# An attention and feed-forward layer on eight cores: the feed-forward weights quantised with their input channels on the partitions

## The chip, the cores and the metric

The kernel runs on all 8 NeuronCores of one Trainium2 chip, each on its own 1024 of the 8192 tokens; no core waits for another. The time is that of the slowest core, in microseconds (us). The engines are TensorE (PE: matmuls and, by matmul with an identity, transposes), VectorE (DVE), ScalarE (ACT), GpSimd (POOL, here only an issuer of DMAs) and SyncE (SP, the other issuer of DMAs). Each runs its own list of instructions in order and waits on semaphores.

## The reference

With D = 2048 channels and 16 heads of 128, cut to what matters:

```
x = x + attention(layernorm(x), w_qkv) @ w_proj.T      # softmax over the 16 heads of one token
z  = layernorm(x)
xq = fake_quant(z, 8, axis=-1)         # scale = max|.| / 127, round(z / scale) * scale
kq = fake_quant(kernel, 8, axis=0)     # one scale for each OUTPUT channel, over all input channels
y  = relu(xq @ kq + fake_quant(bias))
x  = x + fake_quant(y, 8, axis=-1)
```

`kernel` is [2048 input channels, 2048 output channels] in float32. Its quantised form `kq` depends on no activation, so each core can make it any time before the last matmuls.

## The kernel before

**Start.** SP loads the 8 token tiles (128 tokens x 2048, 1 MB each). VectorE takes the statistics of a tile, ScalarE normalises it to bf16 (`abuf`), TensorE transposes it in two halves of 8 blocks (`a_transpose`), and `at_evac` copies the first half by VectorE and the second by ScalarE to `aT`. Batches of small matmuls on zeros (`warm`, L938) fill the waits of TensorE between the first tiles. Job 0 starts on tiles 0 to 2 (`q_tiles(0, 0, 3)`), then does tile 3.

**Projection.** 96 jobs: job (e, h) multiplies weight block e of 48 (q, k and v, 16 blocks each) with half h of the tokens, 16 matmuls of 512 columns. POOL loads the weight blocks through six buffers `wqb` with a cast to bf16, block e as soon as the jobs of block e-6 are done, so about 12 jobs ahead. Results lie in five PSUM banks in turn; VectorE evacuates the even jobs, ScalarE the odd ones. In POOL's list the chunks of the output projection's weights (`wpq`) are mixed in.

**Weight quantisation, beside the projection.** Between evacuations, panel by panel: 16 panels of 128 rows of the transposed kernel, so that an output channel lies on one partition and its scale is one number per partition. A panel takes three jobs from job 10 on: VectorE `k_scale` (absolute maximum over 2048, scale, reciprocal), ScalarE `k_round` (multiply and round, in place), VectorE `k_quant` (back to bf16), then SP spills it to DRAM (`kr_spill`).

**Attention.** TensorE runs slots, written out by the loop `for sl in range(NS)`: in slot `sl` the scores of group sl (32 groups), the transposes of sl-1, the product with V of sl-2, and beside them 16 matmuls of the jobs left over (slots 0 to 5), of the output projection (slots 6 to 37, tile b in slots 6+4b to 9+4b) or of the feed-forward product (`y_part`, from slot 38). SP's list holds, in this order and for one after the other: the DMA transposes of V (`v_transpose`, V of tile b), the loads of the residual (`xres_load`, into the space of K and V that are done with; VectorE adds to it in `p_evac`), twelve DMA transposes of the spilled panels (`k_transpose`, which POOL writes back to `kq_spill`), four more straight into `kq[0]` (`kq0_transpose`), the DMA transposes of the quantised activations (`l_transpose`), and then the bias and the loads of `kq[1]`, `kq[2]`, `kq[3]` (`kq_load`, 2 MB each). `kq[1]` to `kq[3]` take the space of `wpq`, so `kq_load(u)` waits for product 28+u of 32 of the output projection.

**Feed-forward.** 32 products `y_part(k, u)` of 16 matmuls; the four of tile k use the four quarters `kq[0]` to `kq[3]` in turn. Then VectorE and ScalarE quantise each tile, and SP stores it.

## Time and profile before

| | us |
|---|---|
| three timed runs | 642.28, 643.17, 647.33 (median 643.17) |
| the profiled execution | 647.92 |
| its span on the slowest core (core 5) | 646.4 |
| spans of cores 0 to 7 | 645.4, 640.6, 636.3, 643.0, 640.5, 646.4, 639.7, 633.5 |
| mean granted TensorE clock of cores 0 to 7 | 0.977, 0.980, 0.988, 0.982, 0.980, 0.981, 0.986, 0.989 |
| TensorE busy on core 5 | 608.7 (94%) |
| VectorE, ScalarE busy on core 5 | 316.8 (49%), 239.4 (37%) |
| on the chain that ended last | TensorE 67%, SP's DMA issues 23% |

The profiled execution lasted 1.5 us longer than the span of its slowest core. TensorE is busy nearly all the time, so the microseconds that can move are those in which it waits or runs at its lower clock. All cores run the same program on equal amounts of work, yet their spans lie 13 us apart; comparing them stage by stage tells which waits made the slow ones slow.

### The profile page before, as it was taken

What the parts mean: (1) busy time and instruction counts of PE and PEld (TensorE: products, weight loads), DVE (VectorE), ACT (ScalarE), POOL (GpSimd) and SP (SyncE); (2) the same over time, 40 slices, a digit from 0 to 9 for tenths busy, and PEclk for the clock granted to TensorE, in tenths of its full rate; (3) what the DMA queues carried; (4) which work ended last, traced back from release to release, by engine and by line L of the source; (5) the groups of instructions that cost most, each with busy time, mean ns of one, the idle gap of its engine ahead of it and who ended that gap; (6) DMA issues with size and microseconds to landing.
All of it is one profiled execution on the core that took longest, in us unless ns stands there. A gap on an engine that the chain in (4) does not pass through costs nothing.

```text
span 646.4 us, 9466 instructions; the slowest of 8 cores (633.5 to 646.4 us)
## 1 busy us (share of the span) xinstructions
PE 608.7 (94%) x3416; PEld 302.7 (47%) x3416; DVE 316.8 (49%) x492; ACT 239.4 (37%) x492; POOL 41.0 (6%) x80
## 2 busy tenths in 40 slices
PE   5789999999999999999999999999979979999993
PEld 5645444444444444444444555554544424444442
DVE  3853445435354340010012456867748635778657
ACT  3862123221331320100002667675647323453331
POOL 0100100000000011111100000000000000000000
PEclk8899999999999999999999999999989999999997
DMA  8998789999999999999834989999999992332313
GB/s 243 268 202 209 158 207 231 199 255 221 228 227 222 248 175 163 165 151 157 119 61 60 184 143 244 199 179 196 147 251 207 260 321 60 98 97 106 122 66 130
DMA packets 88974, 116.02 MB, mean 179 GB/s; under 512 B 69089, under 2 KB 69089, under 8 KB 85217
## 3 DMA queue, kind: packets, MB, share of 16 engines
q1 hardware_dynamic: 77986, 75.58, 46.2%
q0 software_dynamic: 10944, 39.85, 37.5%
q8 instruction: 28, 0.46, 0.3%
q14 instruction: 16, 0.13, 0.1%
HBM read 109.12 MB, written 23.08 MB: 205 GB/s over the span
## 4 chain that ended last, share of the span: by engine, by line
PE 67%; SPq 23%; DMA 6%; DVE 2%; issue 1%; ACT 1%; DVEq 0%; ACTq 0%; POOLq 0%
PE pF L804 49%; PE pF L909 16%; SPq L263 11%; SPq L253 4%; SPq L240 3%; SPq L272 3%; DMA wqb<-wqkv 2%; DMA xbuf<-x_att 2%; DMA kq<-kq_spill 2%; DVE cols L536 1%; SPq L247 1%; PE pF L928 1%; PE pF L822 1%; ACT aT L403 0%; ACT abuf L397 0%
## 5 line engine op out<-in xcount | busy, mean ns | idle before, releaser
L804 PE MATMUL pF<-aT,wqb 128*128 128x512 bf16 x1504 | 327.1, 379 | 2.0 <-DMA wqb<-wqkv 2.0
L804 PEld LDWEIGHTS pF<-aT,wqb 128*128 128x128 bf16 x1504 | 146.5, 98 | 176.2 <-issue 2.3
L886 PE MATMUL pF<-wpq,qT 128*128 128x512 bf16 x512 | 120.9, 382 | 0.0
L909 PE MATMUL pF<-kq,xqT 128*128 128x512 bf16 x496 | 108.8, 382 | 4.8 <-DMA kq<-kq_spill 3.6
L909 PEld LDWEIGHTS pF<-kq,xqT 128*128 128x128 bf16 x496 | 48.6, 98 | 65.1 <-issue 7.9
L886 PEld LDWEIGHTS pF<-wpq,qT 128*128 128x128 bf16 x512 | 48.1, 99 | 48.1 <-issue 1.6
L428 ACT ACTIVATE Ebuf<-pF,cols 128x128 bf16<-128x128 f32 x128 | 45.6, 369 | 40.7 <-DVE cols L598 39.6
L560 DVE CAST vT<-pF 128x512 bf16<-128x512 f32 x16 | 11.0, 690 | 80.8 <-PE pF L804 80.8
L354 POOL DMA_DIRECT2D wqb<-wqkv x48 | 26.0, 541 | 295.5 <-PE pF L804 244.3
L560 DVE CAST kT<-pF 128x512 bf16<-128x512 f32 x16 | 11.1, 692 | 63.0 <-PE pF L804 63.0
L661 DVE SCALAR_TENSOR_TENSOR tt<-pF,cols,bqb 128x512 f32<-128x512 f32 x31 | 23.2, 750 | 38.1 <-PE pF L909 37.9
L415 ACT CAST vT<-pF 128x512 bf16<-128x512 f32 x16 | 9.4, 588 | 83.0 <-PE pF L804 83.0
L415 ACT CAST kT<-pF 128x512 bf16<-128x512 f32 x16 | 9.4, 587 | 80.1 <-PE pF L804 80.1
L557 DVE TENSOR_SCALAR qT<-pF 128x512 bf16<-128x512 f32 x16 | 11.1, 691 | 55.2 <-PE pF L804 49.1
L584 DVE TENSOR_REDUCE cols<-wkf 128x1 f32<-128x2048 f32 x16 | 36.4, 2277 | 0.0
L412 ACT ACTIVATE qT<-pF 128x512 bf16<-128x512 f32 x16 | 9.6, 599 | 71.9 <-PE pF L804 71.9
L419 ACT ACTIVATE wkf<-wkf,cols 128x2048 f32<-128x2048 f32 x16 | 32.0, 2003 | 5.3 <-DVE cols L566 5.3
L468 ACT ACTIVATE tt<-tt,cols 128x2048 f32<-128x2048 f32 x7 | 14.0, 2003 | 48.1 <-DVE cols L566 48.1
L617 DVE TENSOR_TENSOR xr<-pF,xr 128x512 f32<-128x512 f32 x32 | 21.9, 684 | 15.9 <-DMA xr<-x_res 11.2
L598 DVE TENSOR_REDUCE cols<-pF 128x4 f32<-128x512 f32 x32 | 22.0, 688 | 14.5 <-PE pF L844 14.5
L428 ACT ACTIVATION_READ_ACCUMULATOR Ebuf<-pF,cols 128x1 f32 x128 | 26.3, 206 | 0.0
L449 ACT ACTIVATE zb<-xr,cols 128x1024 f32<-128x1024 f32 x16 | 18.6, 1161 | 17.8 <-DVE qx L651 17.8
...
## 6 DMA issues: line engine op xcount, KB each, us to landing
wqb<-wqkv POOLq DMA_DIRECT2D x48, 512.0 KB, 8.6
...
kr_spill<-kqr SPq DMA_DIRECT2D x16, 512.0 KB, 11.3
wpq<-wp POOLq DMA_DIRECT2D x16, 512.0 KB, 9.6
...
kq_spill<-kst POOLq DMA_DIRECT2D x12, 512.0 KB, 8.8
```

The costliest lines, as they stand in the source:

```text
L253: inc(sync.dma_start_transpose(xqT[:, 2048 * b:2048 * (b + 1)].rearrange("p (c n) -> p c n", c=NC), qx[:, :]), f"lT{b}", 16)
L263: inc(sync.dma_start_transpose(kst[i % 5].rearrange("p (c n) -> p c n", c=NC), d_kr[512 + 128 * i:512 + 128 * (i + 1), :]), f"kT{i % 5}", 16)
L354: inc(g.dma_start(wqb[e % NW][:, :], d_wqkv[128 * e:128 * (e + 1), :]), f"wL{e % NW}", 16)
L419: inc(s.activation(wkf[ft % 2][:, :], wkf[ft % 2][:, :], AF.Copy, bias=MAGIC, scale=cc(C_KR[ft])), "kZ")
L428: i = s.activation(Ebuf[g % 2][:, cs], pF[3 + g % 2][:, cs], AF.Exp, bias=cc(C_NM[g % 2] + j), accum_out=cc(C_DEN[g % 2] + j))
L560: inc(v.tensor_copy(qkv_dst(e, h), qkv_src(j)), "qEvV")
L584: h = inc(v.reduce_max(cc(C_KA[ft % 2]), wkf[ft % 2][:, :], AX.X, apply_absolute_value=True), "vS")
L598: inc(v.tensor_reduce(cc(C_NM[g % 2], 4), pF[3 + g % 2].rearrange("p (j n) -> p j n", j=4), AX.X, ALU.max, negate=True), "vMx")
L661: return inc(v.scalar_tensor_tensor(tt[k % 2][:, cs], pF[(4 * k + u) % 4][:, :], cc(C_SX[k]), bqb[:, cs], ALU.mult, ALU.add), "yEv")
L804: mm = tn.matmul(pF[QBANK[j]][:, :], wqb[e % NW][:, 128 * c:128 * (c + 1)], aT[:, 8192 * h + 512 * c: 8192 * h + 512 * (c + 1)], start=(c ...
L886: mm = tn.matmul(pF[SLOTB[f % 3]][:, :], sT[:, 2048 * b + 128 * m: 2048 * b + 128 * (m + 1)], wpq[u][:, 512 * m:512 * (m + 1)], start=(m = ...
L909: mm = tn.matmul(pF[y % 4][:, :], xqT[:, 2048 * k + 128 * c: 2048 * k + 128 * (c + 1)], w[:, c, :, :], start=(c == 0), stop=(c == NC - 1))
```

## The change

The kernel matrix comes in another layout from the host: panel ft holds, on partition p, the 128 output channels n with their 16 input blocks c side by side, so the input channels lie on the partitions. A quantised panel is then already what `y_part` reads. All 16 DMA transposes of panels, `kr_spill` and POOL's twelve write-backs go; SP writes each panel to `kq_spill`, and `kq[0]` is loaded like the others. An output channel's maximum now goes over partitions: VectorE reduces to `kM`, transposes 32x32 blocks, reduces, gathers four lanes, and spreads scale and reciprocal back over all partitions (`kRow`); the multiplication by the reciprocal is a VectorE instruction (`k_mult`), ScalarE only rounds, reading with a stride of 16 elements into a new buffer `wkz`. Panels start at job 4 and take four jobs each, and `k_quant` of a panel stands at the start of the next panel. The buffers move to the space of `wpq[0]` to `wpq[2]`, so the `wpq` loads are spread anew, and POOL waits for the last spills before that of block 39. The residual is loaded from ScalarE's list, after the exponentials of slot 4b+3. At the start, tile 2 is copied by VectorE alone, tile 3 is transposed after `q_tiles(0, 0, 3)`, and one `warm` batch is gone.

```diff
...
-PREP0 = 10
+PREP0, PREPN = 4, 4
...
+WP_WITH = {20: (0, 0), 23: (0, 1), 26: (1, 0), 29: (1, 1), 39: (0, 2), 40: (0, 3),
+           41: (1, 2), 42: (1, 3), 43: (2, 0), 44: (2, 1), 45: (2, 2), 46: (2, 3)}
...
+    wkf = [A(f"wkf{i}", [128, 2048], F32, offset=163840 + 8192 * i)
            for i in range(2)]
-    kqr = [A(f"kqr{i}", [128, 2048], BF16, offset=114688 + 4096 * i)
+    kqr = [A(f"kqr{i}", [128, 2048], BF16, offset=155648 + 4096 * i)
            for i in range(2)]
+    wkz = A("wkz", [128, 2048], F32, offset=139264)
...
-            sync.wait_ge(S_("qMM"), 3)
-            inc(sync.dma_start(wkf[1][:, :], d_bias.partition_broadcast(128)),
+            sync.wait_ge(S_("qMM"), 4)
+            inc(sync.dma_start(wkf[0][:, :], d_wk[0:128, :]), "kL0", 16)
+            inc(sync.dma_start(wkf[1][:, :], d_wk[128:256, :]), "kL1", 16)
+            sync.wait_ge(S_("qMM"), 5)
+            inc(sync.dma_start(bia[:, :], d_bias.partition_broadcast(128)),
...
             sync.wait_ge(S_("bQ"), 1)
-            inc(sync.dma_start(d_bq[:, :], wkf[1][0:1, :]), "bSt", 16)
-            sync.wait_ge(S_("bSt"), 16)
-            inc(sync.dma_start(wkf[1][:, :], d_wkT[128:256, :]), "kL1", 16)
+            inc(sync.dma_start(d_bq[:, :], bia[0:1, :]), "bSt", 16)
             for ft in range(NC):
-                sync.wait_ge(S_("kQ"), ft + 1)
+                sync.wait_ge(S_("kZ"), ft + 1)
                 if ft + 2 < NC:
                     inc(sync.dma_start(
                         wkf[ft % 2][:, :],
...
-                inc(sync.dma_start(d_kr[128 * ft:128 * (ft + 1), :],
-                                   kqr[ft % 2][:, :]), f"kSp{ft % 2}", 16)
...
+                u, f4 = ft // 4, ft % 4
+                sync.wait_ge(S_("kQ"), ft + 1)
+                inc(sync.dma_start(
+                    d_kq[128 * u:128 * (u + 1), 2048 * f4:2048 * (f4 + 1)],
+                    kqr[ft % 2][:, :]), f"kSp{ft % 2}", 16)
...
-            def k_transpose(i):
-                if i == 0:
+            def kq_load(u):
+                if u == 0:
+                    sync.wait_ge(S_("kSp0"), 128)
+                    sync.wait_ge(S_("kSp1"), 128)
                     sync.wait_ge(S_("qMM"), NJ)
-                if i >= 5:
-                    sync.wait_ge(S_(f"kSt{i % 5}"), 16 * (i // 5))
-                inc(sync.dma_start_transpose(
-                    kst[i % 5].rearrange("p (c n) -> p c n", c=NC),
-                    d_kr[512 + 128 * i:512 + 128 * (i + 1), :]),
-                    f"kT{i % 5}", 16)
-            def kq0_transpose(f):
-                sync.wait_ge(S_(f"kSt{f}"), 16 * (3 if f < 2 else 2))
-                inc(sync.dma_start_transpose(
...
-            def kq_load(u):
-                sync.wait_ge(S_("pMM"), 28 + u)
-                if u == 1:
...
-            v_transpose(0)
-            v_transpose(1)
-            xres_load(0)
-            v_transpose(2)
-            k_transpose(0)
-            k_transpose(1)
-            xres_load(1)
-            k_transpose(2)
-            k_transpose(3)
-            v_transpose(3)
-            k_transpose(4)
...
+            for b in range(5):
+                v_transpose(b)
+            kq_load(0)
...
             v_transpose(5)
-            l_transpose(0)
-            k_transpose(8)
-            xres_load(4)
-            k_transpose(9)
             v_transpose(6)
...
             v_transpose(7)
-            kq0_transpose(2)
-            xres_load(6)
-            kq0_transpose(3)
             l_transpose(2)
-            kq0_transpose(0)
-            xres_load(7)
-            kq0_transpose(1)
             sync.wait_ge(S_("tO"), NG)
+            sync.wait_ge(S_("bSt"), 16)
...
-                if 33 <= e < 45:
-                    wp_load((e - 33) // 4, (e - 33) % 4)
+                if e == 39:
+                    g.wait_ge(S_("kSp0"), 128)
+                    g.wait_ge(S_("kSp1"), 128)
+                if e in WP_WITH:
+                    wp_load(*WP_WITH[e])
...
-            for i in range(12):
-                u, f4 = 1 + i // 4, i % 4
-                g.wait_ge(S_(f"kT{i % 5}"), 16 * (i // 5 + 1))
-                inc(g.dma_start(
-                    d_kq[128 * u:128 * (u + 1), 2048 * f4:2048 * (f4 + 1)],
-                    kst[i % 5][:, :]), f"kSt{i % 5}", 16)
...
                 s.wait_ge(S_("qMM"), j + 1)
-                if e == 32:
-                    s.wait_ge(S_("kSp0"), 128)
-                    s.wait_ge(S_("kSp1"), 128)
+                if e == 16:
+                    s.wait_ge(S_("bSt"), 16)
...
                 s.wait_ge(S_("kSc"), ft + 1)
-                inc(s.activation(wkf[ft % 2][:, :], wkf[ft % 2][:, :], AF.Copy,
-                                 bias=MAGIC, scale=cc(C_KR[ft])), "kZ")
+                if ft >= 1:
+                    s.wait_ge(S_("kQ"), ft)
+                inc(s.activation(wkz.rearrange("p (c n) -> p c n", c=NC),
+                                 wkf[ft % 2].rearrange("p (n c) -> p c n", c=NC),
+                                 AF.Copy, bias=MAGIC), "kZ")
...
+            def xres_load(b):
+                s.wait_ge(S_("tS"), 4 * b + 4)
+                s.wait_ge(S_(f"vT{b}"), 16)
+                inc(s.dma_start(
+                    xr_tile(b), d_xres[128 * b:128 * (b + 1), :].rearrange(
+                        "p (h c) -> p h c", h=2)), f"xrL{b}", 16)
...
-            at_evac(2)
...
-                ft, ph = (j - PREP0) // 3, (j - PREP0) % 3
-                if ph == 1 and 0 <= ft < NC:
+                ft, ph = (j - PREP0) // PREPN, (j - PREP0) % PREPN
+                if ph == 2 and 0 <= ft < NC:
                     k_round(ft)
...
+                if sl < NG and sl % 4 == 3:
+                    xres_load(sl // 4)
...
+            def at_evac(t, both=False):
                 v.wait_ge(S_("aT"), 2 * t + 1)
                 src = pH[0][:, :].rearrange("p (c n) -> p c n", c=8)
                 inc(v.tensor_copy(at_dst(t, 0), src), "aEvV")
+                if both:
+                    v.wait_ge(S_("aT"), 2 * t + 2)
+                    src = pH[1][:, :].rearrange("p (c n) -> p c n", c=8)
+                    inc(v.tensor_copy(at_dst(t, 1), src), "aEvS")
...
             def k_scale(ft):
                 v.wait_ge(S_(f"kL{ft % 2}"), 16 * (ft // 2 + 1))
-                h = inc(v.reduce_max(cc(C_KA[ft % 2]), wkf[ft % 2][:, :], AX.X,
+                w3 = wkf[ft % 2].rearrange("p (n c) -> p n c", c=NC)
+                h = inc(v.reduce_max(kM[:, :], w3, AX.X,
                                      apply_absolute_value=True), "vS")
                 wt(v, h)
-                scale_of(cc(C_KA[ft % 2]), cc(C_KS[ft]), cc(C_KR[ft]), "kSc")
+                h = inc(v.transpose(kMT[:, :], kM[:, :]), "vS")
+                wt(v, h)
+                h = inc(v.tensor_reduce(
+                    kSm[:, 0:4], kMT.rearrange("p (j n) -> p j n", j=4), AX.X,
+                    ALU.max), "vS")
+                wt(v, h)
+                for q in range(1, 4):
+                    h = inc(v.tensor_copy(kSm[0:32, 4 * q:4 * q + 4],
+                                          kSm[32 * q:32 * q + 32, 0:4]), "vS")
+                wt(v, h)
+                h = inc(v.tensor_reduce(
+                    kSm[0:32, 16:20],
+                    kSm[0:32, 0:16].rearrange("p (q j) -> p j q", q=4), AX.X,
+                    ALU.max), "vS")
+                wt(v, h)
+                h = inc(v.tensor_scalar(kSm[0:32, 20:24], kSm[0:32, 16:20], Q,
+                                        GUARD, ALU.mult, ALU.max), "vS")
+                wt(v, h)
+                h = inc(v.reciprocal(kSm[0:32, 24:28], kSm[0:32, 20:24]), "vS")
+                wt(v, h)
+                for q in range(1, 4):
+                    h = inc(v.tensor_copy(kSm[32 * q:32 * q + 32, 20:28],
+                                          kSm[0:32, 20:28]), "vS")
+                wt(v, h)
+                h = inc(v.tensor_copy(
+                    kE.rearrange("p (j n) -> p j n", j=8),
+                    kSm[:, 20:28].unsqueeze(2).broadcast_to([128, 8, 32])),
+                    "vS")
+                wt(v, h)
+                return inc(v.transpose(kRow[:, :], kE[:, :]), "vS")
+            def k_mult(ft, h):
+                wt(v, h)
+                w3 = wkf[ft % 2].rearrange("p (n c) -> p n c", c=NC)
+                rb = kRow[:, 128:256].unsqueeze(2).broadcast_to([128, 128, NC])
+                inc(v.tensor_tensor(w3, w3, rb, ALU.mult), "kSc")
 
             def k_quant(ft):
                 v.wait_ge(S_("kZ"), ft + 1)
                 if ft >= 2:
                     v.wait_ge(S_(f"kSp{ft % 2}"), 16 * (ft // 2))
-                inc(v.tensor_scalar(kqr[ft % 2][:, :], wkf[ft % 2][:, :], MAGIC,
-                                    cc(C_KS[ft]), ALU.subtract, ALU.mult), "kQ")
+                inc(v.scalar_tensor_tensor(
+                    kqr[ft % 2].rearrange("p (c n) -> p c n", c=NC),
+                    wkz.rearrange("p (c n) -> p c n", c=NC), MAGIC,
+                    kRow[:, 0:128].unsqueeze(1).broadcast_to([128, NC, 128]),
+                    ALU.subtract, ALU.mult), "kQ")
...
-            at_evac(2)
+            at_evac(2, both=True)
...
-                if j == PREP0 - 4:
+                if j == 6:
                     bias_quant()
-                ft, ph = (j - PREP0) // 3, (j - PREP0) % 3
+                ft, ph = (j - PREP0) // PREPN, (j - PREP0) % PREPN
+                if ph == 0 and 1 <= ft <= NC:
+                    k_quant(ft - 1)
                 if ph == 0 and 0 <= ft < NC:
-                    k_scale(ft)
-                if ph == 2 and 0 <= ft < NC:
-                    k_quant(ft)
+                    h_ks = k_scale(ft)
+                if ph == 1 and 0 <= ft < NC:
+                    k_mult(ft, h_ks)
...
-            for t in range(4):
+            for t in range(3):
                 a_transpose(t)
-                if t < 3:
+                if t < 2:
                     warm(24)
             q_tiles(0, 0, 3)
+            a_transpose(3)
...
-    WkT = np.ascontiguousarray(np.asarray(L0_ffn_kernel, dtype=np.float32).T)
+    Wk = np.asarray(L0_ffn_kernel, dtype=np.float32).reshape(NC, 128, NC, 128)
+    Wk = np.ascontiguousarray(Wk.transpose(2, 1, 3, 0)).reshape(D, D)
...
```

The first matmuls on TensorE (`aTT` are the zeros of `warm`; L791 transposes, L822 and L804 are jobs), before:

```order
L938 MATMUL pF<-aTT_59 128x128 x24
L791 MATMUL pH<-ident,abuf_74 128x128 x16
L938 MATMUL pF<-aTT_59 128x128 x24
L791 MATMUL pH<-ident,abuf_75 128x128 x16
L822 MATMUL pF<-aT,wqb_51 128x384 x16
L822 MATMUL pF<-aT,wqb_51 128x128 x16
L804 MATMUL pF<-aT,wqb_52 128x512 x16
```

and in the changed kernel:

```order
L955 MATMUL pF<-aTT_59 128x128 x24
L808 MATMUL pH<-ident,abuf_74 128x128 x16
L839 MATMUL pF<-aT,wqb_51 128x384 x16
L808 MATMUL pH<-ident,abuf_75 128x128 x16
L839 MATMUL pF<-aT,wqb_51 128x128 x16
L821 MATMUL pF<-aT,wqb_52 128x512 x16
```

The transposes of tile 3 moved behind the 384 columns of job 0, and a batch of 24 is missing.

SP's queue at the end of the attention stage, before (L240 V, L247 residual, L253 activations, L263 and L272 panels):

```order
L263 DMA_TRANSPOSE kst_90<-kr_spill 128x16x128
L240 DMA_TRANSPOSE V_87<-vT 128x16x128
L272 DMA_TRANSPOSE kq_82<-kr_spill 128x16x128
L247 DMA xr<-x_res 128x2x1024
L272 DMA_TRANSPOSE kq_82<-kr_spill 128x16x128
L253 DMA_TRANSPOSE xqT<-qx 128x16x128
L272 DMA_TRANSPOSE kq_82<-kr_spill 128x16x128
L247 DMA xr<-x_res 128x2x1024
L272 DMA_TRANSPOSE kq_82<-kr_spill 128x16x128
L327 DMA bqb<-bq_spill 128x2048
L282 DMA kq_83<-kq_spill 128x8192
L253 DMA_TRANSPOSE xqT<-qx 128x16x128
```

and in the changed kernel:

```order
L251 DMA_TRANSPOSE V_94<-vT 128x16x128
L257 DMA_TRANSPOSE xqT<-qx 128x16x128
L288 DMA bqb<-bq_spill 128x2048
L268 DMA kq_90<-kq_spill 128x8192
L257 DMA_TRANSPOSE xqT<-qx 128x16x128
L268 DMA kq_91<-kq_spill 128x8192
L268 DMA kq_92<-kq_spill 128x8192
```

Between the V transposes and the bias only the activations' transpose is left; the order from the bias on is the same.

One panel on VectorE, before (L557 evacuates a job):

```order
L557 TENSOR_SCALAR qT<-pF 128x64x8
L584 TENSOR_REDUCE cols<-wkf_76 128x1
L563 TENSOR_SCALAR cols<-cols 128x1
L566 RECIPROCAL cols<-cols 128x1
L557 TENSOR_SCALAR qT<-pF 128x64x8
L593 TENSOR_SCALAR kqr_78<-wkf_76,cols 128x2048
```

and in the changed kernel (L530 evacuates a job):

```order
L605 SCALAR_TENSOR_TENSOR kqr_79<-wkz,kRow 128x2048
L561 TENSOR_REDUCE kM<-wkf_76 128x128
L564 STREAM_TRANSPOSE kMT<-kM 128x128
L566 TENSOR_REDUCE kSm<-kMT 128x4
L571 COPY kSm<-kSm 32x4 x3
L574 TENSOR_REDUCE kSm<-kSm 32x4
L579 TENSOR_SCALAR kSm<-kSm 32x4
L582 RECIPROCAL kSm<-kSm 32x4
L585 COPY kSm<-kSm 32x8 x3
L588 COPY kE<-kSm 128x256
L593 STREAM_TRANSPOSE kRow<-kE 128x256
L599 TENSOR_TENSOR wkf_76<-wkf_76,kRow 128x2048
```

Four instructions a panel became sixteen, three of them over 2048 elements, and they follow one another without an evacuation between them.

## Rows read from the trace of the kernel before

**Rows 1.** Span and mean granted TensorE clock of the fastest core.
```profile
core 7: 633.5 us, clock 0.989
```

**Rows 2.** Two lines of TensorE on cores 7, 6 and (second alone) 5: ns min/median/max, first and last start.
```profile
L843 PE MATMUL pF<-neg,ident x128: 216/219/219, 349.5 to 483.9; 128*128 128x128 bf16 x128
L909 PE MATMUL pF<-kq,xqT x496: 376/379/379, 510.6 to 619.5; 128*128 128x512 bf16 x166
...
L843 PE MATMUL pF<-neg,ident x128: 216/219/219, 354.4 to 488.8; 128*128 128x128 bf16 x128
L909 PE MATMUL pF<-kq,xqT x496: 376/379/379, 515.5 to 625.7; 128*128 128x512 bf16 x166
...
L909 PE MATMUL pF<-kq,xqT x496: 376/379/631, 520.3 to 632.5; 128*128 128x512 bf16 x166
```

**Rows 3.** Waits of TensorE from 300 us on: cores 5 (two rows), 0, 7 (total, times, longest).
```profile
PE pH L853 <- DVE Ebuf L610: 7.7, 7, 3.5
PE pF L909 <- DMA kq<-kq_spill: 3.6, 1, 3.6
...
PE pF L909 <- DMA kq<-kq_spill: 8.0, 2, 7.5
...
PE pF L909 <- DMA kq<-kq_spill: 1.8, 1, 1.8
```

**Rows 4.** Timeline of core 5, 455 to 480 us: start, duration, what, [idle before].
```profile
455.34 8.34 SPq L240 DMA_TRANSPOSE V<-vT  x1
468.64 0.55 SPq L247 DMA_DIRECT2D xr<-x_res  x1
...
476.97 0.69 DVE L617 TENSOR_TENSOR xr<-pF,xr 128x512 f32<-128x512 f32 x1 [5.06 <-DMA xr<-x_res]
```

**Rows 5.** SP's queue before the feed-forward product: core 5, then core 7.
```profile
508.31 0.52 SPq L327 DMA_DIRECT2D bqb<-bq_spill  x1
509.19 0.33 SPq L282 DMA_DIRECT2D kq<-kq_spill  x1
509.62 11.22 SPq L253 DMA_TRANSPOSE xqT<-qx  x1
...
495.75 0.35 SPq L327 DMA_DIRECT2D bqb<-bq_spill  x1
499.47 0.33 SPq L282 DMA_DIRECT2D kq<-kq_spill  x1
499.90 8.06 SPq L253 DMA_TRANSPOSE xqT<-qx  x1
```

**Rows 6.** First jobs on TensorE: core 7 (two rows), core 6.
```profile
28.52 3.65 PE L822 MATMUL pF<-aT,wqb 128*128 128x384 bf16 x32 [0.58 <-DMA wqb<-wqkv]
34.50 3.61 PE L804 MATMUL pF<-aT,wqb 128*128 128x512 bf16 x16 [2.33 <-DMA wqb<-wqkv]
...
35.31 6.45 PE L804 MATMUL pF<-aT,wqb 128*128 128x512 bf16 x16 [3.11 <-DMA wqb<-wqkv]
```

**Rows 7.** Groups by form, core 5: busy us, mean ns | idle before.
```profile
L584 DVE TENSOR_REDUCE cols<-wkf 128x1 f32<-128x2048 f32 x16 | 36.4, 2277 | 0.0
L419 ACT ACTIVATE wkf<-wkf,cols 128x2048 f32<-128x2048 f32 x16 | 32.0, 2003 | 5.3 <-DVE cols L566 5.3
...
L593 DVE TENSOR_SCALAR kqr<-wkf,cols 128x2048 bf16<-128x2048 f32 x16 | 20.4, 1278 | 0.0
...
L674 DVE SCALAR_TENSOR_TENSOR xr<-tt,cols,xr 128x2048 f32<-128x2048 f32 x7 | 16.4, 2345 | 0.0
...
L557 DVE TENSOR_SCALAR qT<-pF 128x512 bf16<-128x512 f32 x16 | 11.1, 691 | 55.2 <-PE pF L804 49.1 <-PE pF L822 6.1
...
L566 DVE RECIPROCAL cols<-cols 128x1 f32<-128x1 f32 x33 | 5.4, 164 | 3.4
```

**Rows 8.** DMA issues of the page: count, KB each, median us from issue to landing.
```profile
wqb<-wqkv POOLq DMA_DIRECT2D x48, 512.0 KB, 8.6
...
kr_spill<-kqr SPq DMA_DIRECT2D x16, 512.0 KB, 11.3
```

66 lines of the change are left out of this document (22 added, 44 removed).

## The prediction

> **What bounds the kernel now.** The page comes first: TensorE is busy 94% of the span, so a gain can only come from the few stretches in which it waits or has its lower clock. The spans of the cores come next: the fastest core needs 633.5 us, 13 us less than the slowest, with a granted clock of 0.989 [rows 1]. The same program on equal work took 13 us longer elsewhere; so I cut the path of a core into stages and read where they differ.
>
> The first score matmul (L843) starts at 349.5 us on core 7 and at 354.4 on core 6, where it is latest of all [rows 2]. Everything before it is start and projection; the projection runs without a gap, so this difference is made in the first 55 us. From the first score to the first feed-forward matmul (L909) is 510.6 - 349.5 = 161.1 us on core 7 and 515.5 - 354.4 = 161.1 on core 6 [rows 2]: that is the attention stage undisturbed. The feed-forward stage, first to last start of L909, is 108.9 us on core 7, 110.2 on core 6 and 112.2 on core 5 [rows 2]. From there to the end of the span is 633.5 - 619.5 = 14.0 us on core 7 [rows 1, 2], and core 6, with its span of 639.7, has the same.
>
> The waits of TensorE name the rest [rows 3]. On core 5 it loses 7.7 us in the attention stage to transposes that wait for VectorE (`Ebuf`), and VectorE had waited for the residual: 5.06 us in the largest case. The load was issued at 468.64, when VectorE would want it at 476.97 - 5.06 = 471.9, and took 8.3 us; one transpose before it in SP's queue had taken 8.34 us to issue [rows 4]. Then, at the turn to the feed-forward product, TensorE waits for `kq`: 1.8 us on core 7, 3.6 on core 5, 8.0 on core 0 [rows 3]. There SP issues the bias, `kq[1]`, one activations' transpose and only then `kq[2]` and `kq[3]`; the transpose holds SP for 11.22 us on core 5 and 8.06 on core 7. What differs is the bias before it: on core 5 it was held up behind the panels' transposes and went out 0.9 us before `kq[1]`, on core 7 3.7 us before [rows 5].
>
> **The change part by part.**
> *Panels without DMA transposes.* Sixteen DMA transposes leave SP's queue and twelve write-backs leave POOL's. In the attention stage SP then holds 8 transposes of V and the activations' ones, each ready well before it is needed (V of a tile is issued four slots ahead). What this is worth is the 7.7 us of core 5, and on cores 6 and 7, which had no such wait, nothing: their 161.1 us is the floor. Behind it the bias goes out when the last product with V is done, one product of 16 matmuls before `kq[1]`, which is core 7's spacing on every core. I therefore take the `kq` wait of core 7, 1.8 us. The bounds are 0 (the queues are emptier than on any core now) and 8.0 (core 0's, if the wait is the transfer's and not the order's). The value is nearest to core 7's row, since there the panels' transposes were already finished before the bias. `kq_load(1)` itself cannot go earlier; it waits for its space. For the latest core I take 109.5, between 108.9 and core 6's 110.2.
> *Residual from ScalarE's list.* Eight issues; on SP one takes 0.55 us [rows 4]. Scores and exponentials have about a slot of slack, so 0.55 in one slot of four is hidden; all eight exposed would be 4.4 us. The load is now issued in slot 4b+3 and used in slot 4b+7, four slots of 161.1 / 38 = 4.24 us later, 17 us, against the 8.3 that it takes. Its wait for V's transpose of the same tile is long over by then. Nothing is queued behind it but the copies of the same slot.
> *Vector work in the projection.* One panel on VectorE is now: `k_quant`, a scalar_tensor_tensor over 2048 float32 (nearest row L674, 2.35 us; it was a tensor_scalar of 1.28), a maximum (2.28), thirteen small instructions and a product over 2048 (as L674, 2.35). A small one costs 0.164 plus a gap of 3.4 / 33 = 0.10 us [rows 7]; four work on 128 or 256 columns, bounded by 0.16 and the 0.69 of a 512-column one. Taken together 3.7 us, between 3.4 and 5.6. With one evacuation (0.69) and ScalarE's rounding (2.00), which the next `k_quant` waits for, the loop is 2.35 + 2.28 + 3.7 + 2.35 + 0.69 + 2.0 + 0.3 for gaps = 13.7 us. Four jobs of 16 matmuls last 13.8 (a job is 3.45). It fits, barely. The evacuation behind this burst ends some 12.4 us after the panel's first, where its bank is wanted at 20.7, so 8.3 us of debt cost TensorE nothing. The early panels start late, since the bias's five instructions and the first load come between; the slack covers that too. So: 0.
> *Weight loads.* POOL waits at block 39 for the last spills. These land 0.69 + 2.35 + 11.3 = 14 us or 4 jobs after job 68, so block 40 goes out near job 72 and lands 8.6 us later [rows 8], at job 75; it is wanted at job 80. 0.
> *The start.* Job 0 began at 28.52 us on core 7 because block 0 of the weights landed then, and job 1 waited 2.33 us for its weights [rows 6]. Starting job 0 before tile 3 gains at most 0.6 us and gives it back at job 1. Moved behind the 384 columns, the transposes of tile 3 and their copies (about 1.1 + 1.1 us) now lie between the parts of job 0: 28.3 + 2.6 + 2.2 + 0.9 = 34.0, still before the weights of job 1 at 34.5. At the low clock job 0's 3.5 us of matmuls would be 6.9, and job 1 would start at 37.4. The last batch on zeros is gone, so TensorE idles about 4 us before job 0, and low clock is more likely there; but cores have a low stretch in the start now: core 6 ran job 1 in 6.45 us instead of 3.61 after idling 3.11 [rows 6], and job 2 waits for weights until about 41. Bounds -1 and +3; I take 0.
> The Trainium skill (TensorE: Matmul & The Clock Gate, section "Why this matters for your kernels") wants TensorE kept free of long idle gaps between bursts, since one of them brings the clock down to its half level. The row of core 6 agrees; by that rule taking out the batch costs what rival C says.
>
> **The sum.** The latest core of the changed kernel: first score 353.3 (between core 7's 349.5 and core 6's 354.4, near the upper end since the slowest core counts), + 161.1 + 109.5 + 14.0 + 1.5 (what the execution lasts beyond its slowest span, 647.92 - 646.4) = **639.4**, rounded to 639. Against the profiled execution's 647.9 that is 8.9 less; against the median of the runs, 643.17, it is 4.2 less (0.6%). The profiled execution was a slow one by 4.8 us, and most of that was the waits that go. A change under 1% (6.4 us) counts here as none that a measurement of this kernel can tell.
>
> **Rivals.**
> *A, cleaner than forecast:* the latest first score is at 351 and the `kq` wait is zero (107.1): 351 + 161.1 + 107.1 + 14.0 + 1.5 = 634.7. For it: emptier queues, and half the cores are that early now. Against it: eight cores draw a start each, and the latest counts.
> *B, the `kq` wait stays:* it is the 6 MB that TensorE is waiting for, not SP's order. Feed-forward 112.2 to 116: 642 to 646. For it: SP's order from the bias on is unchanged [rows 5], and every core has the wait. Against: its length follows the spacing of bias and `kq[1]`.
> *C, the start is slower:* the idle time before job 0 brings the low clock to job 0 and again later; +2 to +3: 641.5.
> *D, slower than before:* VectorE's panel loop is longer than four jobs. It decides at 13.8 + 8.3 / 15 = 14.35 us a panel; beyond that evacuations come too late and job j+5 waits for its bank. Were ScalarE's strided rounding 4.0 us instead of 2.0, the loop would be 15.7, the debt 15 x 1.9 = 28, less 8.3: +20, 659. At 3.0 it would be +5, 644. Against: VectorE and ScalarE now write `qT` in scattered runs at ordinary prices (691 ns for 512 [rows 7]).
> The Trainium skill (SBUF — State Buffer, section "Specifications (TRN2)") says that each access that goes to a new 16-byte line pays a penalty; a stride of 64 bytes does so at every element. No row here reads in this way; by that rule D is what happens.
> *E, the change does not do what it says* (the residual still late because ScalarE is busy): 647, with little for it.
>
> **Chances.** Forecast 0.44 (its own range 636.8 to 641.5), A 0.27, B 0.13, C 0.08, D 0.06, E 0.02. The range 634.5 to 645.5 takes in A, C and most of B and leaves out D, E and the outer ends. Faster by over 1% (below 636.7): A and a fifth of the forecast, 0.36. Slower by over 1% (above 649.6): D and ends of B and E, 0.07. Within 1%: 0.57.
>
> **What the profile would show.** Right: no wait of VectorE on the residual and none of TensorE on `Ebuf` on any core; 161.1 us from the first score to the first L909 on all eight; the bias 3.5 us before `kq[1]`, and a `kq` wait under 2 us; spans closer together than 13 us; no gap of TensorE between job 5 and the first score. Wrong, if first scores come later than 354.4 (C or D: in C the delay stands before job 5, in D after it), or if the `kq` wait is 3 us or more beside an early bias (B).

## The result, and the profile after

The changed kernel takes **650.46 us** (median of 10 runs, 649.15 to 651.68) where the kernel before, run beside it, takes 647.11 (median of 10, 642.28 to 728.61). The ratio is 1.0073, 95% interval 1.0042 to 1.0103: slower, by less than the 1% that counts as a change, and 11 us above the forecast of 639 and outside its range. Medians here and below are of all runs and ratios of the undisturbed ones alone; in experiments 1 to 4 cores 4 to 7 ran at a lower clock than the others in nearly all runs, those of the kernel before too, so their whole times say little and their stages are read on cores 0 to 3.

| stage | before, over the cores | after, over the cores | forecast |
|---|---|---|---|
| first score matmul, from the span's start | 349.0 to 354.4 | 358.0 to 361.6 | 353.3 |
| of it: last matmul of job 4's 128-column part to the first score | 294.6 on all | 301.6 to 303.5 | 294.6 |
| first score to first feed-forward matmul | 161.1 to 171.3 | 161.1 on all | 161.1 |
| first to last start of the feed-forward matmul | 108.9 to 117.7 | 109.9 to 112.9 | 109.5 |
| from there to the span's end | 13.9 to 14.4 | 13.7 to 14.0 | 14.0 |

The head of the page and the groups that matter in it (core 7, the slowest; columns as in [rows 1], [rows 7]):

```profile
span 648.8 us, 9715 instructions; the slowest of 8 cores (643.2 to 648.8 us)
PE 611.1 (94%) x3392; PEld 301.9 (47%) x3392; DVE 408.5 (63%) x685; ACT 262.7 (40%) x491; POOL 34.1 (5%) x68
...
L821 PE MATMUL pF<-aT,wqb 128*128 128x512 bf16 x1504 | 329.7, 379 | 5.3 <-DVE kT L533 3.5
...
L379 ACT ACTIVATE wkz<-wkf 128x2048 f32<-128x2048 f32 x16 | 58.8, 3676 | 156.1 <-DVE wkf L599 156.1
...
L605 DVE SCALAR_TENSOR_TENSOR kqr<-wkz,kRow 128x2048 bf16<-128x2048 f32 x16 | 36.7, 2291 | 41.6 <-ACT wkz L379 41.6
L599 DVE TENSOR_TENSOR wkf<-wkf,kRow 128x2048 f32<-128x2048 f32 x16 | 36.7, 2292 | 1.7
```

The long instructions of VectorE are as costed or cheaper (2.29 us where I had 2.35), and its thirteen small ones take 4.0 us with their gaps, where I had 3.7. One instruction is far off: ScalarE's rounding (L379) takes **3.68 us**, where the same size took 2.00 before [rows 7]. What differs is how it reads: now every 16th float32, a stride of 64 bytes. VectorE's next quantisation (L605) waits 41.6 us for it in all. One panel in the lists of VectorE and ScalarE on core 7 (start, duration, then the wait ahead):

```profile
104.44 2.29 DVE L605 SCALAR_TENSOR_TENSOR kqr<-wkz,kRow 128x2048 bf16<-128x2048 f32 x1 [2.80 <-ACT wkz L379]
106.65 2.28 DVE L561 TENSOR_REDUCE kM<-wkf 128x128 f32<-128x2048 f32 x1
...
112.88 2.29 DVE L599 TENSOR_TENSOR wkf<-wkf,kRow 128x2048 f32<-128x2048 f32 x1
...
115.32 3.67 ACT L379 ACTIVATE wkz<-wkf 128x2048 f32<-128x2048 f32 x1 [10.09 <-DVE wkf L599]
...
119.16 2.29 DVE L605 SCALAR_TENSOR_TENSOR kqr<-wkz,kRow 128x2048 bf16<-128x2048 f32 x1 [2.79 <-ACT wkz L379]
```

L605 starts at 104.44, 119.16, 133.89 and 148.62: a panel every **14.72 us** (three of the fifteen intervals last 15.1, so the mean is 14.80), while TensorE does four jobs in 13.8. TensorE doesn't feel it at once. Its timeline on core 7, through the projection:

```profile
58.62 145.50 PE L821 MATMUL pF<-aT,wqb 128*128 128x512 bf16 x672
204.65 14.20 PE L821 MATMUL pF<-aT,wqb 128*128 128x512 bf16 x64 [0.53 <-DVE kT L533]
219.73 14.21 PE L821 MATMUL pF<-aT,wqb 128*128 128x512 bf16 x64 [0.87 <-DVE kT L533]
234.46 14.21 PE L821 MATMUL pF<-aT,wqb 128*128 128x512 bf16 x64 [0.52 <-DVE kT L533]
249.19 14.22 PE L821 MATMUL pF<-aT,wqb 128*128 128x512 bf16 x64 [0.52 <-DVE kT L533]
263.93 14.20 PE L821 MATMUL pF<-aT,wqb 128*128 128x512 bf16 x64 [0.51 <-DVE kT L533]
278.66 14.21 PE L821 MATMUL pF<-aT,wqb 128*128 128x512 bf16 x64 [0.53 <-DVE kT L533]
293.39 62.55 PE L821 MATMUL pF<-aT,wqb 128*128 128x512 bf16 x288 [0.52 <-DVE vT L533]
```

For 145 us there is no wait; then the free banks are used up, and TensorE runs at VectorE's pace: rows 14.7 us apart. Seven waits of 0.5 to 0.9 us are shown, 4.0 in all; most of the rest of the loss is inside the rows, which last 14.2 where 64 matmuls should need 13.8. After 293 us the panels are done and the pace is TensorE's own again. The stage is 7 to 9 us longer than 294.6 on all eight cores.

Some 7.0 us of that are the same on all cores. The remainder, up to 1.8 us, stands on cores 0, 3, 4 and 7 alone, and is a second effect of the late panels. On core 0:

```profile
302.28 0.53 POOL L320 DMA_DIRECT2D wpq<-wp  x1 [19.39 <-DMA kq_spill<-kqr]
...
357.12 3.61 PE L821 MATMUL pF<-aT,wqb 128*128 128x512 bf16 x15 [1.62 <-DMA wqb<-wqkv]
```

POOL waits 19.4 us for the last spills and then sends out three blocks of weights and four chunks of `wpq` at once. On this core the eight weight loads from there on take 10.2 to 21.6 us to land, against a median of 8.6 before [rows 8], and TensorE waits 1.6 us for the last of them (0.5, 1.1 and 0.5 on cores 3, 4 and 7).

The later stages did what was forecast, or nearly. From core 6, the fastest, and core 7 (count, least, median and greatest duration, then first to last start):

```profile
L860 PE MATMUL pF<-neg,ident x128: 216/219/219, 358.0 to 492.4; 128*128 128x128 bf16 x128
L926 PE MATMUL pF<-kq,xqT x496: 376/379/379, 519.1 to 629.5; 128*128 128x512 bf16 x166
```
```profile
L860 PE MATMUL pF<-neg,ident x128: 216/219/219, 360.8 to 495.2; 128*128 128x128 bf16 x128
L926 PE MATMUL pF<-kq,xqT x496: 376/379/634, 522.0 to 634.9; 128*128 128x512 bf16 x166
```

519.1 - 358.0 and 522.0 - 360.8 are the 161.1 and 161.2 us of [rows 2]; no core waits on `Ebuf` or on the residual. The feed-forward stage is 110.4 and 112.9 us. TensorE's waits on core 7 (waiting line, releaser: total, number, longest) and SP's queue at the turn to that stage:

```profile
PE pH L808 <- ACT abuf L355: 9.4, 4, 5.7
PE pF L839 <- DMA wqb<-wqkv: 4.5, 1, 4.5
PE pF L821 <- DVE kT L533: 3.5, 6, 0.9
PE pF L926 <- DMA kq<-kq_spill: 3.2, 1, 3.2
```
```profile
486.68 1.55 SPq L257 DMA_TRANSPOSE xqT<-qx  x1
507.13 0.32 SPq L288 DMA_DIRECT2D bqb<-bq_spill  x1
510.52 0.32 SPq L268 DMA_DIRECT2D kq<-kq_spill  x1
510.93 9.78 SPq L257 DMA_TRANSPOSE xqT<-qx  x1
520.80 0.99 SPq L268 DMA_DIRECT2D kq<-kq_spill  x2
```

The bias is 3.4 us ahead of `kq[1]`, as forecast, on every core; yet the transpose still holds SP for 9.8 us, and the wait for `kq` is 3.2 us here and 2.5 to 4.8 over the cores, not 1.8. The transpose before it, issued with nothing in flight on SP's queue, took 1.55 us. How long `kq[1]`, issued at 510.52, took to land:

```profile
DMA to landing us min/median/max: 10.5/10.5/10.5
```

It landed at 521.0, and the transpose had let go of SP at 510.93 + 9.78 = 520.7. So it is on every core of this trace and of every later one: the hold ends 0.2 to 0.5 us before the `kq` load ahead of it lands (0.1 in the kernel before). So `kq[2]`, which stands behind the transpose, goes out only when `kq[1]` has landed.

### The profile page after: what moved, and what is told of

Its sections match the earlier page's. It is cut to its first block, busy times and chain, and to the rows that moved or that the text cites. A ratio compares the mean times of both kernels' runs of the same rounds, so it can differ in the third digit from the quotient of the medians.

```text
span 648.8 us, 9715 instructions; the slowest of 8 cores (643.2 to 648.8 us)
## 1 busy us (share of the span) xinstructions
PE 611.1 (94%) x3392; PEld 301.9 (47%) x3392; DVE 408.5 (63%) x685; ACT 262.7 (40%) x491; POOL 34.1 (5%) x68
## 4 chain that ended last, share of the span: by engine, by line
PE 49%; DVE 20%; DMA 9%; issue 9%; ACT 9%; SPq 2%; DVEq 1%; ACTq 0%; POOLq 0%
PE pF L926 16%; PE pF L903 15%; PE pF L821 11%; ACT wkz L379 8%; DVE kM L561 5%; DVE wkf L599 5%; DMA wqb<-wqkv 4%; DMA xbuf<-x_att 2%; DMA kq<-kq_spill 2%; PE pF L839 2%; SPq L257 2%; DVE kSm L585 1%; PE pF L860 1%; DVE kSm L571 1%; PE pF L861 1%
## 5 line engine op out<-in xcount | busy, mean ns | idle before, releaser
L821 PEld LDWEIGHTS pF<-aT,wqb 128*128 128x128 bf16 x1504 | 145.2, 98 | 183.2 <-issue 13.2
L379 ACT ACTIVATE wkz<-wkf 128x2048 f32<-128x2048 f32 x16 | 58.8, 3676 | 156.1 <-DVE wkf L599 156.1
L926 PE MATMUL pF<-kq,xqT 128*128 128x512 bf16 x496 | 110.2, 386 | 4.3 <-DMA kq<-kq_spill 3.2
L605 DVE SCALAR_TENSOR_TENSOR kqr<-wkz,kRow 128x2048 bf16<-128x2048 f32 x16 | 36.7, 2291 | 41.6 <-ACT wkz L379 41.6
L533 DVE CAST vT<-pF 128x512 bf16<-128x512 f32 x16 | 10.9, 687 | 51.0 <-PE pF L821 51.0
L599 DVE TENSOR_TENSOR wkf<-wkf,kRow 128x2048 f32<-128x2048 f32 x16 | 36.7, 2292 | 1.7
L561 DVE TENSOR_REDUCE kM<-wkf 128x128 f32<-128x2048 f32 x16 | 36.4, 2278 | 0.0
L372 ACT CAST vT<-pF 128x512 bf16<-128x512 f32 x16 | 9.2, 587 | 58.4 <-PE pF L821 58.4
L410 ACT CAST qT<-pF 128x512 bf16<-128x512 f32 x32 | 18.8, 589 | 18.8 <-PE pF L884 18.4
L506 DVE BATCH_NORM_STATS2 cols<-xbuf 128x6 f32<-128x512 f32 x32 | 19.7, 679 | 8.8 <-DMA xbuf<-x_att 8.8
## 6 DMA issues: line engine op xcount, KB each, us to landing
kq<-kq_spill SPq DMA_DIRECT2D x4, 2048.0 KB, 10.9
```

The lines of the kernel that those rows point to most:

```text
L379: inc(s.activation(wkz.rearrange("p (c n) -> p c n", c=NC), wkf[ft % 2].rearrange("p (n c) -> p c n", c=NC), AF.Copy, bias=MAGIC), "kZ")
L561: h = inc(v.reduce_max(kM[:, :], w3, AX.X, apply_absolute_value=True), "vS")
L599: inc(v.tensor_tensor(w3, w3, rb, ALU.mult), "kSc")
L605: inc(v.scalar_tensor_tensor(kqr[ft % 2].rearrange("p (c n) -> p c n", c=NC), wkz.rearrange("p (c n) -> p c n", c=NC), MAGIC, kRow[:, 0:12 ...
L821: mm = tn.matmul(pF[QBANK[j]][:, :], wqb[e % NW][:, 128 * c:128 * (c + 1)], aT[:, 8192 * h + 512 * c: 8192 * h + 512 * (c + 1)], start=(c ...
L926: mm = tn.matmul(pF[y % 4][:, :], xqT[:, 2048 * k + 128 * c: 2048 * k + 128 * (c + 1)], w[:, c, :, :], start=(c == 0), stop=(c == NC - 1))
```

## Experiments

After the result the theories were: **T1**, the strided rounding makes the panel loop longer than four jobs (rival D); **T2**, against it, the loss is the new start (C) or the amount of vector work itself; **T3**, the `kq` wait is SP's order, **T4**, against it, the `kq` bytes (B). Lines quoted are of core 0 unless another is named. Experiments 1 to 4, 5 to 8, 9 to 11 and 12 ran on four different chips, so whole times of different groups are compared by their ratios to the kernel before, which ran beside each.

**1. The stride on the write side.** Of the changed kernel:
```diff
-                inc(s.activation(wkz.rearrange("p (c n) -> p c n", c=NC),
-                                 wkf[ft % 2].rearrange("p (n c) -> p c n", c=NC),
+                inc(s.activation(wkz.rearrange("p (c n) -> p n c", c=NC),
+                                 wkf[ft % 2].rearrange("p (n c) -> p n c", c=NC),
```


> The changed kernel, but ScalarE's rounding of a panel reads wkf in its own order and writes wkz with the stride of 16 elements (the same values in the same places). Theory 1, the strided READ makes the rounding 3.68 us instead of 2.00: now 2.0 us, the panel loop falls from 14.72 to 13.05 us, below four jobs (13.8), no wait of TensorE on VectorE's evacuations (6 or 7 of 0.5 before), first scores 7 us earlier (351 to 354.5), 643 us. Rival 2, any stride of 64 bytes on ScalarE costs the same, read or written: 3.7 us, loop and time unchanged at 650. Rival 3, it is slow because VectorE's two-input instructions use SBUF beside it: 3.7 us whatever the order, 650.

The rounding took 3.73 to 3.75 us, the loop 14.82, the projection 302.7 to 304.4; the whole 658.53, ratio 1.0166 (1.0141 to 1.019). Strided writing costs ScalarE what strided reading does (cores 0 to 3); turning the order of the loops around is no cure.

**2. The stride on VectorE's read.**
```diff
-                inc(s.activation(wkz.rearrange("p (c n) -> p c n", c=NC),
-                                 wkf[ft % 2].rearrange("p (n c) -> p c n", c=NC),
+                inc(s.activation(wkz[:, :], wkf[ft % 2][:, :],
...
-                    wkz.rearrange("p (c n) -> p c n", c=NC), MAGIC,
+                    wkz.rearrange("p (n c) -> p c n", c=NC), MAGIC,
```


> The changed kernel, but ScalarE reads and writes in order, and VectorE's k_quant reads wkz with the stride of 16 elements. Theory 1: rounding 2.0 us, k_quant unchanged at 2.29, loop 13.05, first scores 351 to 354.5, 643 us. Rival 2b, a strided read costs VectorE as much as it did ScalarE (2.29 x 1.84 = 4.2 us): loop 14.9, 651. Rival 3 (contention with VectorE): rounding still 3.7, loop 14.7, 650.

```profile
L604 DVE SCALAR_TENSOR_TENSOR kqr<-wkz,kRow 128x2048 bf16<-128x2048 f32 x16 | 58.0, 3626 | 15.7 <-ACT wkz L379 15.7
...
L379 ACT ACTIVATE wkz<-wkf 128x2048 f32<-128x2048 f32 x16 | 30.6, 1910 | 175.5 <-DVE wkf L598 175.5
```
ScalarE's part fell to 1.91 us, and VectorE's rose from 2.29 to 3.63. The stride has a price wherever it stands: 1.77 us on ScalarE, 1.33 on VectorE. The third rival, that the rounding is slow because VectorE works beside it, falls: its price went with the stride. The loop was 14.30 us, the projection 296.7 to 298.2: 0.4 us less a panel gave back some 5 us. The whole was 659.07, set by cores 4 to 7.

**3. The old start.** The changed kernel with all four tiles transposed ahead of job 0:
```diff
-            for t in range(3):
+            for t in range(4):
...
-            a_transpose(3)
```


> The changed kernel with the start of the kernel before: tile 2 copied by both engines, tile 3 transposed ahead of job 0, three batches of matmuls on zeros. Theory: the idle 4 to 5 us ahead of job 0 brought its clock to half on all eight cores (job 0's 384-column part 4.3 to 5.3 us) and moved job 5 from 56.7 to 57.8 us in the mean over the cores; with the old start the mean is 56.7 again, the latest core anywhere between 56 and 60; time 0 to 1.5 us less, 649.5. Rival, the new start is neutral or gains: 650.5 or more. The panel loop stays at 14.72 us in both.

The projection stayed at 301.3 to 303.7 (ratio of the whole 1.0139, 1.0092 to 1.0186). The last 128 columns of job 4 started at 54.5 to 58.3 us, against 56.3 to 58.9 over the changed kernel's eight cores. T2's first half falls: the start is not where 7 us went.

**4. `kq[2]` ahead of the transpose.** `kq_load(2)` goes ahead of `l_transpose(3)` in SP's list, `kq_load(3)` stays behind it.

> The changed kernel, with the load of kq[2] ahead of the third activations' transpose in SP's list. In the changed kernel that transpose holds SP for 9.2 to 10.8 us and kq[2] goes out 10 us after kq[1]. Theory A, SP's order makes the wait of TensorE on kq (2.5 to 4.8 us): kq[2] goes out 3.5 us after kq[1], the wait falls under 1 us, the feed-forward stage from first to last L926 falls from 109.9 to 112.9 to 108 or less, 647.5 us. Theory B, it is the transfer of 6 MB itself: kq[2] goes out early and lands no earlier, the wait stays or moves to kq[3], 650.

```profile
509.33 3.77 SPq L268 DMA_DIRECT2D kq<-kq_spill  x2
513.20 13.15 SPq L257 DMA_TRANSPOSE xqT<-qx  x1
526.44 0.53 SPq L268 DMA_DIRECT2D kq<-kq_spill  x1
```
Behind two loads instead of one the transpose holds SP 11.7 to 13.2 us, and `kq[3]` goes out at 526. The wait was 2.7 to 6.0 us, the stage 111.1 to 114.9: the wait had moved from `kq[2]` to `kq[3]`. `kq[2]` landed 13.7 us after its issue, at 526.5, and the transpose let go of SP at 526.35, 0.2 us earlier. The totals alone don't separate T3 from T4; the trace says that `kq[3]` was held back until `kq[2]` had landed.

**5. The changed kernel once more**, beside the next three.

> The changed kernel itself, to stand beside the others of this job. All theories: ratio to the kernel before about 1.007, projection stage (last matmul of job 4's 128-column part to the first score) 301.6 us or more against 294.6, rounding 3.68 us.

649.34 us, ratio 1.008 (1.0049 to 1.011); projection 301.7 to 303.4.

**6. The stride kept, the wait for it removed.** The quantisation of a panel moves behind the scaling of the next one, so that ScalarE rounds while VectorE scales; `kRow` has two buffers for it.
```diff
-                if ph == 0 and 1 <= ft <= NC:
-                    k_quant(ft - 1)
                 if ph == 0 and 0 <= ft < NC:
                     h_ks = k_scale(ft)
+                if ph == 0 and 1 <= ft <= NC:
+                    k_quant(ft - 1)
```


> The changed kernel with k_quant of the panel before moved behind k_scale (kRow doubled, since k_scale writes it); every instruction and every stride stays. Theory 1: the panel loop is the chain k_quant, k_scale, k_mult, ScalarE's 3.68 us rounding, k_quant again, 14.72 us; with six us of k_scale between rounding and k_quant, VectorE no longer waits for ScalarE, its work of 11.9 us a panel fits in four jobs (13.8), TensorE's waits on evacuations go, projection stage 294.6, time 7 us below the changed kernel. Rival: VectorE's own work and its burst of evacuations are what is too long, or the rate of loads and spills; then the projection stage stays at 301.6.

Two groups, and TensorE's row, on core 2:

```profile
L380 ACT ACTIVATE wkz<-wkf 128x2048 f32<-128x2048 f32 x16 | 58.8, 3675 | 116.3 <-DVE wkf L600 116.3
...
L606 DVE SCALAR_TENSOR_TENSOR kqr<-wkz,kRow 128x2048 bf16<-128x2048 f32 x16 | 36.0, 2252 | 0.6 <-ACT wkz L380 0.6
```
```profile
57.79 293.26 PE L822 MATMUL pF<-aT,wqb 128*128 128x512 bf16 x1331
```
The rounding is as long as ever, 3.68 us; VectorE waits 0.6 us for it in all instead of 41.6, and TensorE has one unbroken row of 293 us. Projection 294.6 on all eight, the whole **643.39**, ratio 0.9974 (0.9951 to 0.9997). T1 is shown from its other side: not the duration, but that it stood in VectorE's loop. T2's second half falls too: the vector work is all there, and fits.

**7. The same with the old start.**

> As quant_after_scale, and the start of the kernel before. By the first job's cores 0 to 3 the old start brought job 5 forward by 0.6 to 3.3 us, and on one disturbed core it came later than ever (60.8). Theory: mean over the cores 1 to 2 us earlier, the latest core the same within 1 us, so 0 to 1 us below quant_after_scale. If the new start is neutral, no difference.

642.01, ratio 0.9957 (0.9935 to 0.9979). Job 4's last part started at 56.0 us in the mean (54.3 to 58.5) against 57.7 in 6.

**8. The kernel before with the new start alone.**

> The kernel BEFORE with only the new start (tile 2 copied by VectorE alone, tile 3 behind the 384 columns, one batch of matmuls on zeros fewer). Theory: job 0's 384-column part at half the clock (4.3 to 5.3 us) on all cores, mean start of job 5 a good 1 us later than before, the latest core no later (58 to 59), time +0 to +1.5 us. Rival: the new start gains, 1 us or more below before.

646.76, ratio 1.003 (0.9999 to 1.0061); job 4's last part at 57.8 us in the mean, against 56.7. The new start costs the mean core 1.1 us here and 1.7 in 7; the latest core, which counts, comes no later with it (58.8 here against 59.8 before, 58.4 in 6 against 58.5 in 7), and the total here is not told from zero.

**9. All of `kq` ahead of the transpose.** Of 7:
```diff
-            l_transpose(3)
             kq_load(2)
             kq_load(3)
+            l_transpose(3)
```


> quant_after_scale_old_start with kq[1], kq[2] and kq[3] ahead of the third activations' transpose on SP. There TensorE waits 2.5 to 4.5 us for kq and the feed-forward stage is 111.2 to 113.0 us. Theory A (SP's order): the three loads go out 3.5 us apart, the wait falls under 1 us, the stage to 108, time 3 us less, 639. Theory B (the bytes: bias 1 MB and kq 6 MB at some 280 GB/s, DMA share 1.0 from 500 to 525 us): the last of kq lands when it did, since the 0.5 MB of the transpose is all that moved behind; wait 2 to 4 us, time within 1 us of 642, or longer if VectorE then waits for the transpose.

```profile
496.08 0.32 SPq L289 DMA_DIRECT2D bqb<-bq_spill  x1
499.47 7.23 SPq L269 DMA_DIRECT2D kq<-kq_spill  x3
506.79 21.05 SPq L258 DMA_TRANSPOSE xqT<-qx  x2
...
522.53 22.82 PE L928 MATMUL pF<-kq,xqT 128*128 128x512 bf16 x105 [1.10 <-DMA kq<-kq_spill]
...
524.39 0.69 DVE L668 TENSOR_SCALAR qx<-zb 128x1024 bf16<-128x1024 f32 x1 [8.86 <-DMA xqT<-qx]
```
**637.97 us, ratio 0.9904 (0.987 to 0.9938): below both kernels.** The stage is 106.8 to 108.7 us against 111.2 to 113.0 in 7, and the wait 0 to 1.8. The three loads go out 3.4 us apart, as their products are done, and land at 510.2, 516.2 and 522.4; the third transpose lets go of SP at 522.2 (15.4 us; the row above holds the fourth too, issued at 526.4 in 1.4 us). The same bytes, issued sooner: T3 holds, and T4 doesn't explain the 3 us. The price is a wait of VectorE for the transposes, 8.9 us, which TensorE doesn't see.

**10. The bias behind `kq[3]`.** Of 7, the bias's broadcast moves behind the last `kq` load, the transpose stays ahead of `kq[2]`.

> quant_after_scale_old_start with the 1 MB bias broadcast issued behind kq[3] instead of ahead of kq[1]. Theory B (bytes): 1 MB fewer ahead of kq is 1.05 MB / 280 GB/s = 3.7 us, of which the part that was already through when kq[1] went out (3.4 us of head start) doesn't count, so 0.5 to 1.5 us; VectorE's first evacuation waits for the bias for some us, inside the slack of four PSUM banks (13.8 us). Time 0 to 1.5 us below 642. My forecast's idea (the spacing of bias and kq[1] sets how long the transpose holds SP, and with it the wait): the transpose holds SP for 5 us instead of 9 to 10, the wait falls to under 1 us, 3 us less, 639.

```profile
498.49 8.45 SPq L258 DMA_TRANSPOSE xqT<-qx  x1
...
525.44 0.75 DVE L678 SCALAR_TENSOR_TENSOR tt<-pF,cols,bqb 128x512 f32<-128x512 f32 x1 [14.86 <-DMA bqb<-bq_spill]
```
The transpose holds SP 8.1 to 10.9 us over the cores, 9.5 in the mean, where it was 8.3 to 10.5 in 7, also 9.5 in the mean; the wait is 1.7 to 4.7; 642.98, ratio 0.9969 (0.9941 to 0.9997). With no bias ahead of it the hold is no shorter. So the reading of [rows 5], that the spacing of bias and `kq[1]` sets this wait, was wrong. What sets it is that `kq[2]` and `kq[3]` stand behind a transpose which is held until `kq[1]` has landed. On the same chip, 9 is 5 us faster than this.

**11. The kernel before with the residual on ScalarE's list**, and nothing else.

> The kernel BEFORE with one thing changed: the residual is loaded from ScalarE's list after the exponentials of slot 4b+3; the panels' 16 DMA transposes stay on SP. Theory: the attention stage was long (162 to 171 us on some cores) because the residual load stood in SP's queue behind those transposes; now 161.1 to 161.5 on every core and no wait of VectorE on the residual, slowest span 1 to 5 us shorter, 641 to 644. Rival: the transposes also delay V, the activations and the bias, and the DMA engines are full (share 1.0 and over), so the residual lands late from ScalarE as well and some core keeps 163 or more; then only taking the transposes out did it.

Waits on core 4:
```profile
PE pH L848 <- DVE Ebuf L605: 9.8, 4, 5.2
PE pF L862 <- DMA V<-vT: 7.8, 2, 5.5
...
DVE xr L612 <- DMA xr<-x_res: 5.1, 1, 5.1
DVE qx L646 <- DMA xqT<-qx: 10.0, 2, 7.2
```
666.24, ratio 1.0297 (1.0223 to 1.037), and 161.1 to 187.5 us of attention stage. TensorE now waits for V: on core 4 two of V's transposes took 14.5 and 22.4 us from issue to landing, where the same two took 7.6 and 8.4 in the kernel before. Why is not shown; on the slow cores (1, 4 and 7) the panels' transposes go out no earlier than they did. Moving the residual alone is harmful, so the 161.1 on all cores needed the transposes taken out. Whether that would have been enough with the residual left on SP was not tried.

**12. No stride anywhere.** The changed kernel, its activation contiguous on both sides (`wkz[:, :]`, `wkf[ft % 2][:, :]`) and VectorE's part as it is. This leaves the reordering out, so the quantised weights land in the wrong places.

> The changed kernel with ScalarE reading and writing a panel in order and k_quant unchanged, so that no instruction of the panel reads or writes with a stride of 64 bytes; it leaves out the reordering of a panel from output channel first to input block first, so the quantised weights land in the wrong places. Theory 1: rounding 1.91 us instead of 3.68, the loop 14.72 - 1.77 = 12.95 us, under four jobs, projection stage 294.6 us on every core, time 7 us below the changed kernel (649.3 to 650.5): 643. That would say that my forecast's sum for the panel was right in all terms but this one. Rival: some other part of the loop is long too; then the stage stays above 294.6.

On core 2:

```profile
L379 ACT ACTIVATE wkz<-wkf 128x2048 f32<-128x2048 f32 x16 | 30.6, 1911 | 119.6 <-DVE wkf L598 119.6
```
1.91 us, projection 294.6 on all eight, 642.86, ratio 0.9969 (0.9945 to 0.9994): what 6 gives by another way. Between 5 and 12 lie 649.34 - 642.86 = 6.5 us, or 7 by their ratios (1.008 and 0.9969), the price of the stride inside the loop. Nothing else in the changed projection costs anything by itself: the waits for the last weights go with the loop's.

## Why the prediction failed, step by step

**The panel loop.** "It fits, barely ... So: 0" is the step that failed, by one term of its sum: the rounding at 2.00 us. The others held: 2.29 + 2.28 + 2.29 as against 2.35 + 2.28 + 2.35, and from the end of L561 to the start of L599 some 4.0 us (79.17 to 83.14 on core 7) for the small instructions with their gaps and a wait at 3.7. With 3.68 us in place of 2.00 my sum gives 13.7 + 1.7 = 15.4; measured were 14.72. The 0.7 between is the evacuation, which I had added and which runs while ScalarE rounds: from the end of L599 to the next L605 pass 4.0 us, and VectorE idles 2.80 of them. So the loop is 11.0 us and the rounding, and it would have kept up with 13.82 for any rounding up to 2.8. At 3.68 it is behind by 0.9 us a panel, and with the three longer intervals by 14.7 in fifteen; the banks absorbed 7.7 of these (I had 8.3), and TensorE paid 7.0.

**The weight loads**, put at 0, cost up to 1.8 us on four cores, as shown above. The sum had POOL's wait at block 39 right in kind, but took the last spills to come without the loop's delay and the next loads to land in 8.6 us; they took 10.2 to 21.6.

**Rival D** was what happened, and I gave it 0.06. Its point of decision was right: 14.35 us lies below the measured 14.72, and by its formula the measured debt costs 14.7 - 8.3 = 6.4, against 7.0. Its price for a given rounding was not: a rounding of 3.68 gives a loop of 15.4 and + 15 us by that sum, twice what came, because the evacuation was counted on top of it. What was wrong was the evidence against it. [Rows 7] show `qT` written in scattered runs at an ordinary price, and those are runs of several bf16 side by side; no row had an access that jumps 64 bytes at each element. With no row for the pattern, 2.00 was a price for another instruction, and the 3.0 to 4.0 of rival D should have been what I planned with: the margin that I had worked out was 0.1 us.
By the Trainium skill (SBUF — State Buffer, section "Specifications (TRN2)") an access to a new 16-byte line is penalised; runs 1, 2 and 12 agree, 1.91 against 3.68 to 3.75 us on ScalarE and 2.29 against 3.63 on VectorE. I had cited it and still weighed it at a sixteenth.

**The attention stage** was right: 161.1 on all eight cores, no `Ebuf` wait, no wait on the residual; run 11 shows that the move of the residual alone doesn't give this; how much it adds to the first edit is open. The spread of the cores shrank from 13 to 5.6 us. The issues on ScalarE's list cost nothing, as costed.

**The `kq` wait** was forecast at 1.8 us and came at 2.5 to 4.8, the stage at up to 112.9 instead of 109.5. The observed signature is rival B's (3 us or more beside an early bias), its mechanism is not: run 9 took the wait away by order alone. What failed here is the reading of [rows 5], that the hold follows the spacing of bias and `kq[1]`: in every trace it follows the landing of the load ahead, which took 8 us or more each time, bias or no bias. Core 7's 1.8 us was the shortest wait of eight, and with that reading gone nothing spoke for taking it for the latest core.

**The start** cost 1.1 us in the mean. Job 0's first part took 4.3 to 5.3 us on all eight cores, where five had 2.8 before. On core 7 (stretches of TensorE: stretch and its length, busy time and count, granted clock, DMA's share and rate; then a row of its timeline):
```profile
26.00:27.00 1.00, 0.00 (x0) 0.50 0.96 238
...
31.00:32.00 1.00, 1.00 (x5) 0.50 1.03 238
...
33.00:34.00 1.00, 1.00 (x11) 1.00 1.00 283
```
```profile
29.63 4.27 PE L839 MATMUL pF<-aT,wqb 128*128 128x384 bf16 x16 [4.50 <-DMA wqb<-wqkv]
```
TensorE idled 4.5 us, and the granted clock fell to half, 1.2 GHz, and was back at 2.4 GHz from 33 us on. The idling of rival C is there, at half its price: job 1 had waited 2.33 us for its weights in [rows 6] and doesn't wait now, so part of the delay lies in what was idle time. To the slowest core it cost 0 (58.9 against 59.8), as taken.

**The sum.** On core 7, the slowest: 360.8 + 161.2 + 112.9 + 13.9 + 1.6 (what the execution lasts beyond the span) = 650.4, against 639.4. Of the 11.0 us between, 7.5 are the first score, which is the loop (with 0.5 of the weights' wait), and 3.4 the feed-forward stage with its `kq` wait. Run 6, with the loop out of the way, gave 643.39, inside the range.

The sign was wrong because the change took up to 10 us of the attention stage from the cores that had waited there, and laid 7 to 9 us on every core. Such a trade looks like no change in the total, and only the stages show that both halves are real.
